# A bias matmul replaced by GpSimd adds, idle experts' sums split over two stages, and routing rows placed in waits

## What is computed

```python
# layer 1 attention, per block of 128 tokens; 16 heads of 64
q = (query @ Wq + bq); k = key @ Wk + bk; v = value @ Wv + bv
out = softmax(q @ k.T / 8) @ v
y = out @ Wo + bo
x3 = layernorm(y + residual) * gamma + beta        # then normalised again for the router
# layer 1 experts: top-1 routing
e = argmax(z @ Wr + br)
h = relu(z @ W1[e] + b1[e])
result = h @ W2[e] + b2[e]   # and what the seven experts that get a zero row add
```

## Time and profile before

| | |
|---|---|
| runs, median (lowest to highest) | 1408.55 us (1407.53 to 1410.29), 3 runs |
| the profiled execution | 1411.97 us, its span 1410.2 us |
| PE busy | 1325.4 us, 94% of the span |
| DVE busy | 1121.3 us, 80% |
| ACT busy | 1034.7 us, 73% |
| POOL busy | 378.6 us, 27% |
| mean granted clock of PE | 0.974 |

### The profile page before, as it was taken

One profiled execution on the slowest core, in us unless ns is written; L12 is line 12 of the kernel. 1 busy time (PEld: TensorE's weight loads), 2 busy tenths in 40 slices (PEclk: granted clock), 3 DMA queues, 4 the chain that ended last, 5 costly groups with the idle time before them and its releaser, 6 DMA issues. The chain is left out here.

```text
span 1410.2 us, 34565 instructions
## 1 busy us (share of the span) xinstructions
PE 1325.4 (94%) x11294; PEld 1144.6 (81%) x11294; DVE 1121.3 (80%) x2018; ACT 1034.7 (73%) x2689; POOL 378.6 (27%) x644
## 2 busy tenths in 40 slices
PE   5999988999999999996899999999999679999998
PEld 3666666778888788995899999999998579999998
DVE  6899976979768796783677877778778758889887
ACT  4888877566589875751788878888887258888886
POOL 5555542000011110013011211112112124554553
PEclk9999999999999999998999999999999679999999
DMA  8411252574278998436023233243320276111110
GB/s 264 128 38 37 91 163 83 166 267 165 75 239 269 314 304 276 165 121 230 28 99 110 92 131 110 84 139 108 137 98 17 99 260 243 54 54 43 53 51 11
DMA packets 103881, 190.99 MB, mean 135 GB/s; under 512 B 12980, under 2 KB 68177, under 8 KB 99156
## 3 DMA queue, kind: packets, MB, share of 16 engines
q1 hardware_dynamic: 90656, 151.85, 32.0%
q0 software_dynamic: 10464, 33.57, 8.2%
q10 hardware_dynamic: 2644, 4.09, 0.9%
HBM read 124.17 MB, written 68.03 MB: 136 GB/s over the span
## 5 line engine op out<-in xcount | busy, mean ns | idle before, releaser
L2298 ACT ACTIVATE c_w_raw<-c_ps_score,c_neg_max 128x128 f32<-128x128 f32 x512 | 182.0, 393 | 36.0 <-DVE c_neg_max L2089 20.6
L2643 PE MATMUL d_ps_hT<-d_zT,d_w_tile 128*128 128x128 f32 x1248 | 147.9, 277 | 2.2 <-DVE d_zT L2756 2.2
L2643 PEld LDWEIGHTS d_ps_hT<-d_zT,d_w_tile 128*128 128x128 f32 x1248 | 144.8, 194 | 2.9 <-DVE d_zT L2756 2.9
L2656 PE MATMUL d_ps_y<-d_w_parts,d_hT 128*128 128x256 f32 x936 | 121.7, 286 | 1.8 <-DVE d_res L2787 1.8
L2298 ACT ACTIVATION_READ_ACCUMULATOR c_w_raw<-c_ps_score,c_neg_max 128x1 f32 x512 | 119.0, 232 | 0.0
L2822 ACT ACTIVATE d_h<-d_ps_hT,d_b1T 128x128 f32<-128x128 f32 x312 | 88.7, 366 | 38.8 <-PE d_ps_hT L2643 38.8
L2656 PEld LDWEIGHTS d_ps_y<-d_w_parts,d_hT 128*128 128x128 f32 x936 | 114.6, 191 | 2.1 <-DVE d_res L2787 2.0
L1946 PE MATMUL c_ps_proj<-c_xnT,ahead_wq 128*128 128x256 f32 x768 | 108.2, 292 | 0.0
L2775 DVE TENSOR_TENSOR d_w_parts<-d_w,d_w_parts 128x1024 fp32r<-128x1024 f32 x78 | 95.4, 1223 | 12.6 <-ACT d_w_parts L2834 12.6
L1946 PEld LDWEIGHTS c_ps_proj<-c_xnT,ahead_wq 128*128 128x128 f32 x768 | 96.3, 191 | 5.0 <-issue 5.0
L1990 PE MATMUL c_ps_aux<-c_wo,c_attnT 128*128 128x256 f32 x768 | 99.4, 286 | 0.0
(11 more groups left out here) (338 smaller groups left out, 3548.9 us busy)
## 6 DMA issues: line engine op xcount, KB each, us to landing
keys_scratch<-b_out SPq DMA_DIRECT2D x64, 256.0 KB, 4.5
values_scratch<-b_out SPq DMA_DIRECT2D x64, 256.0 KB, 3.9
d_w<-w_in SPq DMA_DIRECT2D x16, 1024.0 KB, 7.1
ahead_kT<-keys_scratch SPq DMA_DIRECT2D x15, 1024.0 KB, 6.1
split_scratch<-b_split SPq DMA_DIRECT2D x12, 1024.0 KB, 5.2
c_v_more<-values_scratch SPq DMA_DIRECT2D x24, 512.0 KB, 4.1
a_w<-w_in SPq DMA_DIRECT2D x64, 128.0 KB, 2.6
b_ctx_high<-split_scratch POOLq DMA_DIRECT2D x16, 512.0 KB, 5.3
```

The costliest lines, as they stand in the source:

```text
L2298: last = act.activation(prob[:, n, j, :], ps_score[:, n % 2, j, :], ACT.Exp, bias=neg_max[:, n, j:j + 1], accum_out=row_sum[:, n, j:j + 1])
L2643: last = pe.matmul(ps_hT[:, f, :], w1_tile[:, half, k, n * P:(n + 1) * P], zT[:, s, k, :], start=(k == 0), stop=(k == ND - 1))
L2656: last = pe.matmul(ps_y[:, 0:D], hT[:, s, a, f, :], w2_parts[:, half, b, n, :], start=(f == 0 and (a, b) == PARTS[0]), stop=(f == FB - 1 a ...
```

## The change

In the attention:
- `bo` is no longer added by a matmul in each block. In step 0 PE spreads it once over 128 partitions, ACT copies it to `bo_all`, and POOL adds `bo_all` to `xn` in each block, once the transposition has read `xn`. DVE's `add_residual` waits for that.
- In steps 30 and 31 `turn_z` stands right behind the first scores, and ACT's `copy_z` at the head of its step's copies. Two sums of constant rows are computed in each of these two steps, in ps_proj, ahead of the weighted values. ACT copies them in step 32. The sums' small inputs are loaded at the attention's start.
- Step 32 places the rows of blocks 10 to 16. Block 17 is placed before the last x3, 18 and 19 before the last z, 20 to 24 before the last route, and 25 in the head of `experts`.

In the experts:
- The other four sums are computed behind the first layer and `turn_z` of the first tile and copied by ACT ahead of its rounding of w2. The waits for the sums in front of the first tile are gone; DVE's first `residual` waits for them.
- The first two gathers take their numbers from `ids` itself.
- The tensors w1_tile, w2_parts and h lie first in SBUF, so that `other` can lie where the attention held wq. SP's queue has one small load ahead of the weights instead of three.

```diff
+        bo_all = sb("bo_all", [P, D])
...
+        sums = [ps_proj[:, bank, e * D:(e + 1) * D] for bank in (1, 0) for e in range(2)]
...
+                for n, src in enumerate(idle_rows):
+                    sp.dma_start(prep["constant_rows"][n * NE:(n + 1) * NE], src).then_inc(idle_loaded, 16)
...
+                pool.tensor_scalar(prep["all_but"][:], ident[0:2 * NE, 0:NE], -1.0, 1.0, ALU.mult, ALU.add).then_inc(all_but_ready, 1)
...
+                def add_bias(t, w):
+
+                    pool.wait_ge(xnT_done, t + 1)
+                    pool.tensor_tensor(xn[:, w, :], xn[:, w, :], bo_all[:], ALU.add).then_inc(bias_added, 1)
...
+                        if isinstance(b, int) and b == 0:
+                            pool.wait_ge(bias_copied, 1)
+                        add_bias(b, w)
...
-                        pe.wait_ge(bo_ready, 1)
-                        pe.wait_ge(ones_ready, 1)
-                    pe.matmul(ps_aux[:, 0:D], two_ones[:], bo_parts[:], start=True, stop=False)
                     pe.wait_ge(attnT_ready, 2 * t + 2)
                     for n, (blk, (a, c)) in enumerate(product(range(BLKS), PARTS)):
                         last = pe.matmul(ps_aux[:, 0:D], attnT[:, s, a, blk, :], wo[:, c, blk, :],
-                                         start=False, stop=(n == BLKS * len(PARTS) - 1))
+                                         start=(n == 0), stop=(n == BLKS * len(PARTS) - 1))
...
+                def sums_of_idle_rows(first):
+                    pe.wait_ge(q_ready, BLKS // 2 * NB)
+                    pe.wait_ge(all_but_ready, 1)
+                    pe.wait_ge(idle_loaded, 32)
+                    if first:
+                        pe.wait_ge(ranks_taken, 1)
+                    for e in range(first, first + 2):
+                        last = pe.matmul(sums[e], prep["all_but"][:, e:e + 1].to_broadcast([2 * NE, P]), prep["constant_rows"][:],
+                                         start=True, stop=True)
+                    last.then_inc(summed, 1)
...
+                    unhidden = isinstance(b, int) and NB - 2 <= b < NB
                     turn_of_loop[0] = i
                     if here:
                         scores(b, u, 0, i)
+                    if unhidden:
+                        turn_z(b, u)
...
+                    if isinstance(b, int) and b == 0:
+                        pe.wait_ge(bo_ready, 1)
+                        pe.wait_ge(ones_ready, 1)
+                        pe.matmul(ps_out[:, 0:2, :], two_ones[:], bo_parts[:], start=True, stop=True).then_inc(bias_spread, 1)
...
+                    if unhidden:
+                        sums_of_idle_rows(2 * (b - NB + 2))
                     turned = inside(b, 4, NB) or inside(b, NB + 3, NB + 3)
-                    if turned:
+                    if turned and not unhidden:
...
+                    dve.wait_ge(bias_added, t + 1)
...
                         route(NB - 3)
                         route(NB - 2)
+                        place_rows(17, 18)
...
+                    if isinstance(b, int) and b == NB + 2:
+                        place_rows(18, 20)
+                    if isinstance(b, int) and b == NB + 3:
+                        place_rows(20, LATE - 1)
...
                         normalise_routed(NB - 2, (NB - 2) % 4, None)
-                        place_rows(10, LATE)
+                        place_rows(10, 17)
...
+                    unhidden = isinstance(b, int) and NB - 2 <= b < NB
+                    if unhidden:
+                        copy_z(b - 4)
...
+                    if isinstance(b, int) and b == 0:
+                        act.wait_ge(bias_spread, 1)
+                        act.activation(bo_all[:], ps_out[:, 0:2, :].rearrange("p h k -> p (h k)"), ACT.Copy).then_inc(bias_copied, 1)
+                    if (inside(b, 4, NB) or inside(b, NB + 3, NB + 3)) and not unhidden:
                         copy_z(b - 4)
...
                         copy_z(NB - 3)
                         copy_z(NB - 2)
+                        for n, bank in enumerate((1, 0)):
+                            act.wait_ge(summed, n + 1)
+                            act.activation(prep["other"][:, 2 * n:2 * (n + 1), :],
+                                           ps_proj[:, bank, 0:2 * D].rearrange("p (e d) -> p e d", d=D), ACT.Copy).then_inc(other_ready, 1)
...
+SUMS_EARLY = NE // 2
...
-        ps_other = (ps_hT[:].rearrange("p f t -> p (f t)").rearrange("p (e d) -> p e d", d=D),
-                    ps_y[:].rearrange("p (e d) -> p e d", d=D), ps_zT[:].rearrange("p (e d) -> p e d", d=D))
-        sums = [bank[:, e, :] for bank in ps_other for e in range(bank.shape[1])]
...
+        ps_other = psum("ps_other", [P, NE - SUMS_EARLY, D])
...
-                for dst, src in ((constant_rows[0:NE], idle_dram), (constant_rows[NE:2 * NE], w["b2"]), (b1T[:], w["b1T"])):
-                    sp.dma_start(dst, src).then_inc(bias_loaded, 16)
+                sp.dma_start(b1T[:], w["b1T"]).then_inc(bias_loaded, 16)
...
+                    if inside(j, 2, NT - 1):
+                        pool.wait_ge(zx_ids_ready, ready)
+                        index = zx_ids[:, s:s + 1]
+                    else:
+                        index = ids[:, j:j + 1]
...
                 for j in range(2):
-                    copy_zx_ids(j, j, 0)
                     gather(j, j)
...
-                pe.wait_ge(all_but_ready, 1)
-                pe.wait_ge(bias_loaded, 48)
-                for e in range(NE):
-                    last = pe.matmul(sums[e], all_but[:, e:e + 1].to_broadcast([2 * NE, P]), constant_rows[:], start=True, stop=True)
-                last.then_inc(summed, 1)
...
+                def sums_of_idle_rows():
+                    for e in range(SUMS_EARLY, NE):
+                        last = pe.matmul(ps_other[:, e - SUMS_EARLY, :], all_but[:, e:e + 1].to_broadcast([2 * NE, P]), constant_rows[:],
+                                         start=True, stop=True)
+                    last.then_inc(summed, 1)
...
                     if inside(j, 0, NT - 2):
                         turn_z(j + 1, (s + 1) % NS, i + (s == NS - 1))
+                    if isinstance(j, int) and j == 0:
+                        sums_of_idle_rows()
                     if inside(j, 1, NT):
                         second_layer(j - 1, (s + NS - 1) % NS)
...
-                pe.wait_ge(other_ready, len(ps_other))
...
+                def place_row(t):
+                    dve.tensor_scalar(at_row[:, 0, t, :], numbers16[:], slot_row[:, t:t + 1], token_no[:], ALU.is_equal, ALU.mult)
+                    return dve.tensor_scalar(at_row[:, 1, t, :], numbers16[:], slot_row[:, t:t + 1], float(P * (t - NB)),
+                                             ALU.is_equal, ALU.mult)
+
+                place_row(LATE - 1)
...
+                    if isinstance(j, int) and j == 0:
+                        dve.wait_ge(other_ready, 1)
...
-                dve.wait_ge(other_ready, len(ps_other))
...
+                    if isinstance(j, int) and j == 0:
+                        act.wait_ge(summed, 1)
+                        act.activation(other[:, SUMS_EARLY:NE, :], ps_other[:], ACT.Copy).then_inc(other_ready, 1)
...
-                act.wait_ge(summed, 1)
-                first = 0
-                for bank in ps_other:
-                    n = bank.shape[1]
-                    act.activation(other[:, first:first + n, :], bank, ACT.Copy).then_inc(other_ready, 1)
-                    first += n
-                act.wait_ge(bias_loaded, 48)
+                act.wait_ge(bias_loaded, 16)
...
+        prep["other"] = nc.alloc_sbuf_tensor_at("prep_other", [P, NE, D], F32, offset=ahead_at["wq"])
```

53 lines of the change are left out of this document (29 added, 24 removed).

## The result

| | before | after |
|---|---|---|
| median (lowest to highest), 4 runs each | 1409.42 us (1407.53 to 1410.72) | 1391.68 us (1388.89 to 1396.51) |
| the profiled execution, its span | 1411.97, 1410.2 us | 1389.98, 1388.2 us |
| PE busy in the span | 1325.4 us | 1304.1 us |
| POOL busy | 378.6 us | 399.4 us |
| mean granted clock of PE | 0.974 | 0.983 |

The ratio is 0.9879, with a 95% interval from 0.9846 to 0.9911: 17.7 us less by the medians, where 16.75 were forecast.

What follows compares the result with a forecast made beforehand. PE was taken to bound the attention blocks, with ACT 0.29 us in hand, and DVE's rows the attention's end. Terms 8.7 + 0 + 1.5 + 3.35 + 3.3 - 0.1 = 16.75 off 1408.55 gave 1391.8 us; range 1387 to 1398.5.

Steps and rivals of the forecast that it cites:

- A: Attention blocks: bias matmul removed; PE frees 0.31 us, ACT allows 0.29, over 30 blocks 8.7 us gained (3.9 to 9.3).
- PE still idle nowhere: Sign for the attention blocks: with the bias matmul gone and blocks 0.3 us shorter, PE would still have no idle time.
- A reading of mine: Attention, port lock: no row of before has a DVE operation with two SBUF inputs side by side with a POOL add.
- B: Blocks 30 and 31: four sum passes hidden in PE's wait, z turned early; 1.5 us gained (1.0 to 2.7).
- The order of z: Block 31: with z copied early, scores wait for the exponentials alone and add_residual comes 1.5 us earlier.
- The sentence on the clock: Block 31: the filled gap keeps PE's clock up, making the gain 1.5 us and not 1.0.
- C: Step 32: nine of sixteen placed rows move into DVE's waits, freeing the finished product; 3.35 us gained (2.9 to 3.5).
- D: Expert head: sixteen passes leave PE, token numbers start 3.05 us earlier, the first layer 3.3 (2 to 3.9).
- E: First tile: four sums behind its first layer fill PE's 1.72 us wait; cost 0.1 us (-1.2 to +3).
- The fourth gather: First tiles: PE already waits 1.16 us for it; sharing DMA engines with earlier loads might make it 1.1 us later.

Runs made afterwards that it cites:

- a_alone: Before with only the bias matmul out of all blocks (one spread and copy, a POOL add per block): 1399.81 us, ratio 0.9926.
- act_order: After with ACT copying the previous block's second attention half ahead of the first queries, in every step: 1388.70 us, ratio 0.9845.
- z_back: After with z's transposition and ACT's copy of it back at their old place in blocks 30 and 31: 1390.96 us, ratio 0.9873.
- best: After with ACT's second attention half copied ahead of the first queries and the four later sums moved to the expert head: 1390.00 us, ratio 0.9868.
- best2: After with ACT's second attention half copied ahead of the first queries and z's old order in blocks 30 and 31: 1387.75 us, ratio 0.9856.
- fill: After with eight more, unneeded sum passes on PE in step 32, in its 2.22 us wait for DVE's division: 1395.56 us, ratio 0.9892.
- rows_alone: Before with only nine of step 32's sixteen placed rows moved into DVE's waits of steps 32 to 35 and the expert head: 1407.35 us, ratio 0.9980.
- sums16: After with the four later sums, each made twice (sixteen passes), in the expert head and none in tile 0: 1396.48 us, ratio 0.9923.
- no_add: After with POOL's add of the bias left out in all blocks, its signal kept: 1394.90 us, ratio 0.9893.

## Why the prediction held, and which steps of it didn't

**A, 8.7 us: right, for the reason given.** 0.293 us a block from block 3 to block 30 in after, 0.291 in a_alone, which is 8.8 and 8.7 for 30 blocks. I had taken the smaller of what PE frees (0.31) and what ACT allows (0.29). ACT's figure came from one block and a handover of 0.06 us read elsewhere. Over blocks 3 to 29 the gap from ACT's last exponential to PE's scores was 0.38 us on average before and is 0.10 after, a difference of 0.285. PE freed more: from the transpositions' start to the product's it was 1.02 + 0.31 us, now 0.85, so 0.48. ACT's 0.29 decided. The mark "PE still idle nowhere" was therefore wrong: it idles 0.12 us a block on average (0.18 in the row at 875.56). With act_order's exchange of ACT's copies nearly all of that idle time goes, and the block is 0.15 us shorter. A reading of mine was wrong beside it: before does have rows in which a DVE operation with two inputs in SBUF starts within a POOL instruction. DVE's L2096 at 809.40 lies in L1889 (808.78 to 809.68) and takes 0.69 us, as elsewhere.

**B, 1.5 us: the time came, its cause was another.** The order of z was to give it and the filled gap to keep the clock. `add_residual` of block 30 does come 1.83 and 1.78 us earlier. But a_alone, without part B, has 1.88, and z_back, without the early z, loses 0.17. What before lost here is DVE's wait of 1.37 us for scores at half clock, 2.08 instead of 1.16. In after, a_alone and z_back the fall doesn't lie on these scores, and then DVE's own queue is what is late, whatever z does. Where the fall does lie on them, the early z hides 0.8 us (best against best2). So the mechanism exists, but it isn't what gave this gain. The sentence on the clock failed most plainly. It fell to 0.50 behind a better filled PE, some 9 us later. The Trainium skill (TensorE: Matmul & The Clock Gate, Part 1) says that activity releases the throttle; here it did not hold off a fall, as fill shows.

**C, 3.35 us: right, and the shortfall lies ahead of it.** The rows did stand in a finished product's way: its wait fell from 3.24 us to 0.20 in after (0.1 was forecast) and by 3.20 in rows_alone. The moved rows cost little, too: from `add_residual` of block 31 to the experts it is 7.85 us, before 7.78. Yet the stretch gave 4.24 and 4.05 where 5.14 were forecast (B and C 4.85, and one block of A). The product itself isn't as early as I put it: in after the clock's fall lies ahead of it, on the weighted sums (1.97 instead of 1.09). In act_order, without that fall, it starts 1.07 us earlier. In rows_alone the fall lies on the product and takes 1.5, which leaves 2.43.

**D, 3.3 us: right.** 3.34 and 3.24 between the first and the second pair of traces. Of the 3.05 forecast for the numbers (3.06 and 3.30 measured), 2.2 are the passes (sums16), and the rest agrees with the load that PE had to wait for, which the prediction didn't name.

**E, cost 0.1: right within the scatter.** The sums exactly fill the wait (7.74 us from first layer to first layer, 7.80 before). The first pair of traces showed a gain of 1.8 from tile 0 to tile 11; the second pair shows a loss of 1.0. The fourth gather, my doubt, went the other way: in the four traces with the old head PE waits 1.67, 0.75, 1.55 and 0.34 us for gathers in tiles 1 to 8, in the nine with the new head and at most eight passes 0 twice, 0.17 to 0.44 six times, and 1.53. That is some 0.7 us less on average, while the whole of tiles 0 to 11 is 0.4 us shorter on average (75.5 against 75.9), less than it scatters. Which of the edits to the loads does it I haven't tried.

The sum of the means: 29 blocks of 0.293 up to the scores of block 30, so 8.5, then 4.15 + 3.3 + 0.4, makes 16.35 us against 16.75. The medians say 17.7 and 18.1; the rest is within what the stage ahead of the second attention scatters. That B's term came in full is luck: its cause wasn't the one given. The 0.9 to 1.1 us by which a new fall of the clock cut the end of the attention short was in part made up by E, whose cost of 0.1 came out as a gain within its scatter.

What stays open is what makes the clock fall in steps 30 to 32, and so why it no longer lies on the scores of block 31. In two executions each of before and after it came at the same place, and filling one wait didn't shift it. But the code of the attention alone doesn't fix it: act_order and best have the same attention, and their first falls come 40.5 and 18.5 us behind the scores of block 30.

## What to carry to other kernels

Price a removed instruction by what the next engine allows, not by its own length, and look for that engine at once when the gain is in: here an exchange of two ACT copies gave another 4 us from block 3 to block 30. Read terms by stretches between landmarks, and run both kernels a second time: the stage that wasn't touched moved by 4 us, and a gain of 1.8 us in the first tiles turned into a loss of 1.0. An edit taken back alone says what it is worth where the other effects happen to lie: the early z was worth 0.2 us in one kernel and 0.8 in another. A term that rests on the clock staying up needs its own bound in both directions, since a fall moves with the schedule and costs only where it meets work that others wait for.

## What the hardware showed that I hadn't expected

- The granted clock falls to 0.50 in the last 30 us of an attention in which PE had been busy 99 us in 100 or more, in 13 of 14 traces. In these the first fall lies 18.5 to 31.6 us behind the scores of block 30 (before: 19.3 twice; after: 28.1 and 27.7). In the fourteenth, act_order's, it comes 40.5 us behind them.
- The price of a fall: on the last product 4.59 to 4.61 us in four kernels and 5.17 in no_add, against 2.98 to 3.10; on 16 weighted-sum records 1.97 against 1.09.
- A POOL addition of 128x256 makes the DVE operation of the same size beside it 0.033 us longer (509 against 476 ns).
- Kernels with the same attention blocks differ by 0.6 us in 27 blocks (354.16 to 354.77); after, run twice, repeats within 0.1 us.
